# Rows of v from VectorE's 32 by 32 transposes, levels scaled per group, and another order of loads

## What is computed

```python
# cond: weight + LoRA delta, quantised per group of 128 to 8 codebook levels
lora_delta = lora_B @ lora_A * (32.0 / 64)
cb    = codebook / max(|codebook|)
scale = exp(scale_log)                               # (512, 4, 1)
norm  = (weight + lora_delta).reshape(512, 4, 128) / scale
quantized = cb[searchsorted((cb[:-1] + cb[1:]) / 2, norm)]
xc = x @ (quantized * scale + lora_delta).T
# attention, one head of 128, over 128 keys
q, k, v = split(xc @ Wqkv + bqkv)
x = x + (softmax(q @ k.T / sqrt(128)) @ v) @ Wo + bo
# cond2: base product and two of 8 experts of rank 16
logits = x @ Wr.T + 5 * one_hot(language)
gates  = softmax over the top 2 of the logits
m = x @ W.T + 2 * einsum(x @ A, gates, B)
# ffn with an 8-bit weight
out = x + m @ (ffn_scale * (qweight - zero_point)).T + bias
```

## Time and profile before

| | us |
|---|---|
| median of 3 runs | 107.56 (107.47 to 108.09) |
| the profiled execution | 107.76 |
| its span, first to last instruction | 105.8 |
| TensorE busy | 101.3 |
| VectorE busy | 67.9 |
| ScalarE busy | 52.1 |
| POOL busy | 31.8 |

### The profile page before, as it was taken

The page is one execution under the profiler, slowest core; times in us unless marked ns, Lnnn a source line. Parts: engine busy times, 40 slices in busy tenths (PEclk is TensorE's granted clock), DMA queues, the critical chain, the costliest instruction groups (busy, mean ns, idle before and its releaser), DMA issues.

```text
span 105.8 us, 1459 instructions
## 1 busy us (share of the span) xinstructions
PE 101.3 (96%) x513; PEld 84.1 (79%) x513; DVE 67.9 (64%) x163; ACT 52.1 (49%) x92; POOL 31.8 (30%) x40
## 2 busy tenths in 40 slices
PE   6999999999999999999999999999999999999980
PEld 6748568889788899899888786888898888888850
DVE  0199899889999999525999753014946802572441
ACT  4077898999989932934222239272037204002000
POOL 4000246799709570399000056400000400000000
PEclk9999999999999999999999999999999999999999
DMA  1999999960000000000000000000000640000083
GB/s 40 338 344 301 410 400 406 404 253 0 0 3 0 0 0 0 9 0 0 0 0 0 0 0 0 6 0 0 0 0 0 237 160 0 6 0 0 3 297 99
DMA packets 4599, 9.83 MB, mean 93 GB/s; under 512 B 752, under 2 KB 1008, under 8 KB 4592
## 3 DMA queue, kind: packets, MB, share of 16 engines
q1 hardware_dynamic: 4448, 9.48, 24.6%
q10 hardware_dynamic: 144, 0.26, 0.6%
HBM read 7.64 MB, written 2.10 MB: 92 GB/s over the span
## 4 chain that ended last, share of the span: by engine, by line
PE 89%; DMA 4%; DVE 2%; ACT 1%; DVEq 1%; issue 0%
PE psum L860 19%; PE psum L862 19%; PE psum L861 19%; PE psum L885 7%; DMA lora<-in_lora 4%; PE psum L876 3%; PE psum L895 3%; PE psum L910 3%; PE psum L901 3%; PE psum L905 3%; PE psum L1010 2%; PE psum L1031 2%; PE psum L1025 2%; ACT moe L462 1%; PE psum L1017 1%; PE psum L926 1%
## 5 line engine op out<-in xcount | busy, mean ns | idle before, releaser
L662 DVE COPY_PREDICATED cond_work<-cond_work,psum 128x1024 f32<-128x1024 int32 x10 | 13.7, 1366 | 1.1 <-ACT cond_work L363 0.7
L860 PE MATMUL psum<-G_hi,xT_hi 128*128 128x512 f32 x32 | 12.7, 398 | 0.0
L862 PE MATMUL psum<-G_hi,xT_lo 128*128 128x512 f32 x32 | 12.5, 390 | 0.0
L861 PE MATMUL psum<-G_lo,xT_hi 128*128 128x512 f32 x32 | 12.5, 390 | 0.0
L363 ACT ACTIVATE cond_work<-cond_n,cut_bias 128x1024 f32<-128x1024 f32 x10 | 11.2, 1143 | 0.6 <-DVE cond_n L699 0.6
L578 POOL TENSOR_TENSOR hl<-hl,hl_bias 128x272 f32<-128x272 f32 (+2 forms) x4 | 3.1, 774 | 26.4 <-ACT hl L374 14.4
L523 POOL TENSOR_TENSOR xT_lo<-xT,xT_hi 128x1024 fp32r<-128x1024 f32 x4 | 9.6, 2411 | 3.2 <-DVE cond_work L668 3.2
L860 PE MATMUL psum<-xT_hi,split_b_hi 128*128 128x512 f32 x24 | 9.6, 401 | 0.0
L862 PE MATMUL psum<-xT_hi,split_b_lo 128*128 128x512 f32 x24 | 9.4, 391 | 0.0
L861 PE MATMUL psum<-xT_lo,split_b_hi 128*128 128x512 f32 x24 | 9.4, 390 | 0.0
L885 PE MATMUL psum<-hlT,xT 128*128 128x136 f32 x64 | 8.4, 281 | 0.0
(11 more groups left out here) (166 smaller groups left out, 237.4 us busy)
## 6 DMA issues: line engine op xcount, KB each, us to landing
out<-cond_work SPq DMA_DIRECT2D x7, 256.0 KB, 2.1
cond_n<-in_cond_w SPq DMA_DIRECT2D x2, 512.0 KB, 6.6
xT<-in_x_t SPq DMA_DIRECT2D x2, 512.0 KB, 7.6
q_i<-in_q_t SPq DMA_DIRECT2D x4, 256.0 KB, 7.4
moe<-in_moe_w SPq DMA_DIRECT2D x4, 256.0 KB, 7.4
xT<-in_x_t SPq DMA_DIRECT2D x1, 1024.0 KB, 12.4
wqkv_n<-in_wqkv SPq DMA_DIRECT2D x1, 768.0 KB, 10.3
hlT<-in_hl_t SPq DMA_DIRECT2D x1, 272.0 KB, 5.7
```

Source lines behind the costliest of these rows:

```text
L662: dve.copy_predicated(half(level, h), beyond[n % len(beyond)].bitcast(I32), psum[EARLY][:, j + 1:j + 2].to_broadcast([P, 2 * C])).then_inc ...
L860: pe.matmul(out_ap, l_hi, r_hi, start=first, stop=False)
L861: pe.matmul(out_ap, l_hi, r_lo, start=False, stop=False)
L862: return pe.matmul(out_ap, l_lo, r_hi, start=False, stop=last)
```

## The change

- v's rows. TensorE's `v_rows` and ScalarE's `v_out` go. `v_turn` on VectorE makes them from vT with 16 transposes per half, each of one 32-partition quadrant by 32 columns of 4 batches at once, written to another quadrant. Eight of half 0 stand between `softmax_max(0)` and `softmax_norm(0)`, the other 8 and the 16 of half 1 behind it. `attend` waits for them; `qkv(1, 1, 2)` waits for the copy of vT in place of `v_out`.
- Levels. VectorE makes a table of levels times scales (7 x 16) in bank 7 and the lowest row of it, `floor`; `level` starts from it and `pick` overwrites it with scaled levels per group. `w_eff` becomes one add for each 512 columns. `w_eff_lo` of tiles 0 and 1 goes to POOL (`w_eff_rest`).
- Order. q0 and moe0 load ahead of cond_w0, q2 and moe2 ahead of cond_w1. `w_full(0)` stands ahead of `w_delta_first`; `moe_hi`/`w_hi` and `w_lo` move up by one `beyond_cut` or `pick`. `G_first` stands ahead of `x_hl(0)`, whose result goes to bank 6; delta's tiles 2 and 3 go to banks 4 and 5. The 4 idle turns behind delta go. `scores(1)` stands ahead of `y_o(0)`. `expert_no` is set by VectorE in place of POOL.
- The end. The last batch is stored whole.

```diff
-    FILL = 4
+    DELTA_BANKS = (0, 1, 4, 5)
...
             load("small", small[:, :], small_in)
+            load_proj_weights(0)
             load("cond_w0", cond_n[:, 0:2, :], cond_w[:, 0:2, :])
             load("hlT", hlT[:, :, :], hl_t)
             load("x0", xT[:, 0, :, :], x_t[0])
-            load_proj_weights(0)
             load_proj_weights(1)
+            load_proj_weights(2)
             load("cond_w1", cond_n[:, 2:4, :], cond_w[:, 2:4, :])
-            load_proj_weights(2)
             load_proj_weights(3)
...
-            for b in range(BATCH - 1):
+            for b in range(BATCH):
                 sp.wait_ge(y_ready, b + 1)
                 sp.dma_start(out[b], y_out[:, b, :]).then_inc(stored, 16)
-            b = BATCH - 1
-            for n in range(2):
-                sp.wait_ge(y_ready, b + n + 1)
-                s = slice(n * C // 2, (n + 1) * C // 2)
-                sp.dma_start(out[b, :, s], y_out[:, b, s]).then_inc(stored, 16)
...
+        def v_quads(ap, h, n):
+            return ap[:, h, :].rearrange("p (b n) -> p b n", b=TPH)[:, :, n * QUAD:(n + 1) * QUAD]
...
             delta_out(0)
             delta_out(1)
-            set_level()
             delta_out(2)
             delta_out(3)
+            act.wait_ge(floor_ready, 1)
+            act.activation(by_group(half(level, 0)), floor_of(0), ACT.Copy).then_inc(level_set, 1)
             beyond_cut(0, 0)
-            beyond_cut(1, 0)
             moe_hi(1)
             w_hi(1)
-            beyond_cut(2, 0)
-            hl_raw(0, 4)
+            beyond_cut(1, 0)
             moe_hi(2)
             w_hi(2)
-            beyond_cut(3, 0)
+            beyond_cut(2, 0)
+            hl_raw(0, 6)
             moe_hi(3)
             w_hi(3)
+            beyond_cut(3, 0)
...
-                dve.copy_predicated(half(level, h), beyond[n % len(beyond)].bitcast(I32),
-                                    psum[EARLY][:, j + 1:j + 2].to_broadcast([P, 2 * C])).then_inc(picked, 1)
+                at = GROUPS * j + GROUPS // 2 * h
+                dve.copy_predicated(by_group(half(level, h)), by_group(beyond[n % len(beyond)].bitcast(I32)),
+                                    psum[EARLY][:, at:at + GROUPS // 2].unsqueeze(2).to_broadcast(
+                                        [P, GROUPS // 2, P])).then_inc(picked, 1)
...
-                for g in range(CT * o, CT * (o + 1)):
-                    ins = dve.scalar_tensor_tensor(g_block(level, g), g_block(level, g), scale[:, g:g + 1],
-                                                   g_block(delta, g), ALU.mult, ALU.add)
-                ins.then_inc(w_eff_ready, 1)
+                dve.tensor_tensor(level[:, o, :], level[:, o, :], delta[:, o, :], ALU.add).then_inc(w_eff_ready, 1)
...
+            w_full(0)
             w_delta_first()
...
-            w_full(0)
+            w_full(1)
             pick(0, 0)
-            w_full(1)
-            pick(1, 0)
             w_lo(1)
             w_full(2)
-            pick(2, 0)
+            pick(1, 0)
             w_lo(2)
             w_full(3)
+            pick(2, 0)
+            w_lo(3)
             pick(3, 0)
-            w_lo(3)
...
+            def v_turn(h, columns):
+                dve.wait_ge(qkvT_ready, 3 + h)
+                for k in columns:
+                    for d in range(QUADS):
+                        dve.transpose(v_quads(v, h, d)[k * QUAD:(k + 1) * QUAD], v_quads(vT, h, k)[d * QUAD:(d + 1) * QUAD])\
+                           .then_inc(v_ready, 1)
...
             softmax_max(0, 3)
+            v_turn(0, range(0, 2))
             softmax_norm(0)
+            v_turn(0, range(2, QUADS))
+            v_turn(1, range(QUADS))
             o_lo(0)
...
-            idle_turns(FILL)
...
+            G_first()
             pe.wait_ge(loaded["hlT"], 16)
-            x_hl(0, 4)
-            G_first()
+            x_hl(0, 6)
             G_product(1)
...
             qkv(1, 2, 0)
-            pe.wait_ge(qkvT_ready, 3)
-            v_rows(0, 2)
-
...
             probs_turn(0, 3)
-            pe.wait_ge(v_ready, 1)
+            pe.wait_ge(qkvT_ready, 3)
             qkv(1, 1, 2)
...
             o_hl(0, 1, 2)
+            pe.wait_ge(qkvT_ready, 6)
+            scores(1, 0)
             pe.wait_ge(oT_hi_ready, 1)
             pe.wait_ge(oT_lo_ready, 1)
-            y_o(0)
-            pe.wait_ge(qkvT_ready, 6)
-            scores(1, 0)
-            for t in range(1, TPH):
+            for t in range(TPH):
                 y_o(t)
...
             x_hl(3, 3, (6, 7))
-            v_rows(1, 2)
```

More of the change, by code:

```diff
@@ L61, in block_kernel @@
     SOFTMAX_SCALE = float(D) ** -0.5
+    QUAD = 32
+    QUADS = P // QUAD
     LORA_COPIES = 2
@@ L94, in block_kernel @@
         levels = sb("levels", [P, LEVELS])
+        floor = sb("floor", [P, GROUPS])
         cuts = sb("cuts", [P, CUTS])
@@ L251, in block_kernel @@
         max_ready = sem("max_ready")
+        v_ready = sem("v_ready")
         probs_ready = sem("probs_ready")
@@ L346, in w_hi @@
                 rounded(split_b_hi[:, o, :], w_ffn[:, o, :], w_hi_ready)
-            def set_level():
-                act.wait_ge(ones_ready, 1)
-                act.wait_ge(levels_ready, 1)
-                act.activation(half(level, 0), ones[:, 0:1].to_broadcast([P, 2 * C]), ACT.Identity,
-                               bias=levels[:, 0:1], scale=0.0).then_inc(level_set, 1)
             def beyond_cut(j, h):
@@ L528, in _ @@
             pool.memset(ones[:, :], 1.0).then_inc(ones_ready, 1)
-            for e in range(E):
-                pool.memset(expert_no[:, e:e + 1], float(e)).then_inc(ident_ready, 1)
             def x_lo(pair):
@@ L555, in _ @@
                 [P, GROUPS // 2, P]), ALU.mult).then_inc(norm_late_ready, 1)
-            pool.tensor_copy(half(level, 1), levels[:, 0:1].to_broadcast([P, 2 * C])).then_inc(level_late_set, 1)
+            pool.tensor_copy(by_group(half(level, 1)), floor_of(1)).then_inc(level_late_set, 1)
             pool.wait_ge(expb_hi_ready, 1)
@@ L561, in _ @@
             x_lo(1)
+            w_eff_rest(0)
             wqkv_rest(0)
-            pool.wait_ge(w_eff_lo_ready, 2)
+            w_eff_rest(1)
             wqkv_rest(1)
@@ L606, in _ @@
             dve.memset(blank[:, :], 0.0).then_inc(blank_ready, 1)
+            for e in range(E):
+                dve.memset(expert_no[:, e:e + 1], float(e)).then_inc(expert_no_ready, 1)
             dve.wait_ge(loaded["small"], 16)
@@ L618, in _ @@
             dve.wait_ge(scale_ready, 1)
+            dve.tensor_scalar(floor[:, :], scale, levels[:, 0:1], None, ALU.mult).then_inc(floor_ready, 1)
             dve.reciprocal(inv_scale[:, :], scale).then_inc(inv_scale_ready, 1)
@@ L693, in _ @@
             alone(dve.tensor_tensor(cuts[:, 2:3], cuts[:, 2:3], cuts[:, 3:4], ALU.min))
+            dve.tensor_tensor(psum[EARLY][:, 0:CUTS * GROUPS].rearrange("p (j g) -> p j g", j=CUTS),
+                              levels[:, 1:LEVELS].unsqueeze(2).to_broadcast([P, CUTS, GROUPS]),
+                              scale.unsqueeze(1).to_broadcast([P, CUTS, GROUPS]), ALU.mult).then_inc(picks_ready, 1)
             dve.tensor_scalar(cut_bias[:, :], cuts[:, :], -CUT_GAIN, None, ALU.mult).then_inc(cut_bias_ready, 1)
+            w_full(0)
             w_delta_first()
@@ L725, in _ @@
             pick(3, 1)
-            w_eff_lo(0)
-            w_eff_lo(1)
             pick(4, 1)
@@ L832, in gh_lo, with y_store @@
                    .then_inc(ghT_lo_ready, 1)
-            def y_store(t, n=slice(0, C)):
+            def y_store(t):
                 dve.wait_ge(y_done, t + 1)
                 dve.wait_ge(y_bias_ready, 1)
-                dve.tensor_tensor(y_out[:, t, n], psum[4 + t % 4][:, n], y_bias[:, n], ALU.add).then_inc(y_ready, 1)
+                dve.tensor_tensor(y_out[:, t, :], psum[4 + t % 4][:, :], y_bias[:, :], ALU.add).then_inc(y_ready, 1)
             softmax_max(0, 3)
+            v_turn(0, range(0, 2))
             softmax_norm(0)
+            v_turn(0, range(2, QUADS))
+            v_turn(1, range(QUADS))
             o_lo(0)
@@ L850, in _ @@
             gh_lo(1, 0)
-            for t in range(TPH, BATCH - 1):
+            for t in range(TPH, BATCH):
                 y_store(t)
-            for n in range(2):
-                y_store(BATCH - 1, slice(n * C // 2, (n + 1) * C // 2))
         @block.tensor
@@ L875, in _ @@
             for o in range(CT):
-                pe.matmul(psum[o][:, :], lora[:, 0, o * P:(o + 1) * P], lora[:, 1, :], start=True, stop=True)\
+                pe.matmul(psum[DELTA_BANKS[o]][:, :], lora[:, 0, o * P:(o + 1) * P], lora[:, 1, :], start=True, stop=True)\
                   .then_inc(delta_done, 1)
-            idle_turns(FILL)
             def x_hl(part, bank, batches=None, base=0):
@@ L1000, in _ @@
             pe.wait_ge(ident_ready, 1)
-            def v_rows(h, bank):
-                for b in range(TPH):
-                    mm = pe.transpose(psum[bank][:, b * P:(b + 1) * P], vT[:, h, b * P:(b + 1) * P], ident[:, :])
```

(1 more changed line is left out.)

42 lines of the change are left out of this document (22 added, 20 removed).

## The result

| | before | after |
|---|---|---|
| median in the timed comparison, us | 107.83 (107.47 to 108.54) | 111.02 (110.75 to 111.16) |
| the profiled execution | 107.76 | 110.75 |
| its span | 105.8 | 108.9 |
| VectorE busy | 67.9 | 76.6 |
| granted clock, mean | 1.00 | 0.984 |

What follows compares the result with a forecast made beforehand. TensorE was taken to bound the kernel nearly everywhere, except in the softmax stretch. The terms -0.1 (start, behind softmax), -0.44 (second v transposes) and +0.1 (end) gave -0.45 us: 107.56 to 107.1 us, range 106.3 to 108.0.

Steps and rivals of the forecast that it cites:

- Step 2: Softmax stage, half 0: eight VectorE transposes at 0.29 us each in 1.58 us idle; probabilities turned at 65.3, not 65.40.
- what is left of step 1 behind step 2: Sum's term at probs_turn(0): of the 0.85 us gained at the start, only 0.1 remains after the softmax stage, so -0.1.
- Step 1: Kernel start: without idle turns G_first begins at 8.31, 0.89 us gained, inputs in time; scores(0) 0.85 us early, at 59.4.
- VectorE becomes the bound of the stage: Rival, softmax_max(0) to o_lo(0): dearer transposes delay reciprocal and gating; 108.2 us at 0.35, 110.8 at 0.43; chance 0.1.
- rule on quadrants: Softmax stage: instructions starting in another quadrant wait for all earlier ones; with 311 ns a transpose, no gain there, sum 107.3.
- Step 3: Second v transposes, between x_hl and y_gh(0) on TensorE's dense line: the whole 0.44 us gained, no wait at y_gh(0).
- Step 4: The end: one whole store in place of two half stores lands at 105.55 in place of 105.45; 0.1 us lost.

Runs made afterwards that it cites:

- kernel 1: After, with both halves' v transposes back on TensorE and ScalarE's copies behind them, rest of the change kept; 107.63 us, ratio 0.9962.
- kernel 2: Before, with only the v transposes moved to VectorE (8, scaling, 24); loads, levels, idle turns and last store as before; 110.87 us, ratio 1.0232.
- kernel 7: After, with 4 transposes in place of 8 ahead of softmax_norm(0), the others behind it; 108.84 us, ratio 1.0069.
- kernel 6: kernel 3 with 16 more VectorE transposes behind its 16, reading and writing quadrant 0 alone, result unused; 107.58 us in one run.
- kernel 8: kernel 3 with moe_lo's four products of G_product(1) ahead of w_lo's; 107.43 us, ratio 0.9926.
- kernel 3: After, with half 0's v transposes back on TensorE and half 1's 16 on VectorE behind the scaling; 107.35 us, ratio 0.9923.
- kernel 4: After, with 12 idle turns of TensorE in the gap ahead of probs_turn(0); 109.19 us, ratio 1.0086.
- kernel 5: After, with POOL's addition of y_bias made to wait until the scaling of the probabilities is done; 108.12 us, ratio 1.000.

## Why the prediction was wrong, step by step

**Step 2 failed, in its price and in what it left out.** The place was right: the softmax chain sets the stage, and the transposes count from 0.197 us each on. The price was 0.29 us "that is no overlap"; it is 0.33. The duration was nearly met (303 ns against 292 from the line through the earlier trace rows), but instructions that don't overlap have a further 0.03 us between them. By the step's own rule the eight cost 2.65 in place of 2.32 us, 0.3 of the loss, and would have turned the probabilities at about 65.6 in place of 65.3 had TensorE come to the stage as forecast, which makes 107.4. The price of 0.33 was inside my bounds of 0.21 to 0.35, so that alone would have left the time within the range. In the sum the term "what is left of step 1 behind step 2" stood at -0.1; at probs_turn(0) it measured +1.85, and with the clock, which the sum lacks, +3.46 at attend(0).

The larger part was in no step. In the stage's sum the scaling was moved as a block of 0.69 us, and what POOL does at that moment wasn't looked at. Two edits brought the two together. The eight transposes moved the scaling 0.8 us later. And the addition moved 0.67 us earlier: 0.2 of it with the whole stage (it begins at 65.86 in kernel 1), and 0.47 since it waits for ScalarE's boG, in front of which the change took away v_rows(0) and v_out(0), ScalarE's copy of v. That is one more consequence I had not followed. The timelines of before and then of after:

```profile
64.68 0.72 POOL L581 TENSOR_TENSOR hl<-hl,lang_hot 128x8 f32<-128x8 f32 x1
65.38 0.60 ACT L497 ACTIVATE boG<-psum 128x512 f32<-128x512 f32 x1
66.06 1.29 POOL L589 TENSOR_TENSOR ffn_bias_bc<-boG,ffn_bias_bc 128x512 f32<-128x512 f32 x1 [0.66 <-ACT boG L497]
```

```profile
64.72 0.59 ACT L493 ACTIVATE boG<-psum 128x512 f32<-128x512 f32 x1
```

Before, the scaling was over at 65.35 and the addition began at 66.06. (Kernel 2 has lost v_out(0) as well, and meets the addition in the same way. In kernel 7, without v_out(0) but with an early scaling, they don't meet. Late transposes with v_out(0) left in were not run.) The trace of before even held two signs that one of these engines can hold up the other. One is the first row above, an operation on 8 columns that begins 0.03 us behind VectorE's scaling and takes 0.72 us; in after, with no scaling beside it, it takes 0.20. The other is w_lo, 0.67 and 0.69 us at its other two places, and 1.01 here beside POOL:

```profile
16.25 1.01 DVE L644 TENSOR_TENSOR split_b_lo<-q_i,split_b_hi 128x512 fp32r<-128x512 f32 x1
```

It is the later one that waits. POOL's subtraction beside this w_lo ran from 15.40 to 16.71, and w_lo ended at 17.26, 0.55 us behind it. The scaling of after ended at 67.20, 0.55 us behind POOL's 66.65, and w_lo(1) of kernel 1 (below) at 14.90, 0.54 us behind 14.36. So these traces give an estimate: a two-input VectorE instruction of this size that begins during one of POOL's ends some 0.55 us after POOL does. That would have given the 1.05 us beforehand.

Then the gap of 2.61 us, its 1.05 from the collision, lowered the clock: another 1.61 us. Neither had a term, a rival or a bound. The stage's prices were bounded one instruction at a time, and that left out what two together do.

**The rival "VectorE becomes the bound of the stage"** had the place and the sign, but the wrong mechanism: it wanted 0.35 to 0.43 us a transpose to reach 108.2 or 110.8, and it got there at 0.33 with the collision and the clock. Its second half held as a threshold: "from 0.32 us the 24 behind the scaling pass the 7.5 + 0.93 us that gating(0) has". In after o_lo(0) starts at 75.26 right behind the last transpose, and gating(0) starts 9.1 us after probs_turn in place of 7.5. It did no harm there, since TensorE was late itself: y_gh(0) comes +3.14 late where attend(0) came +3.46. In kernel 7, where TensorE was on time, that queue did cost (0.23 us at o_lo(0)).

**Of the Trainium skill's rule on quadrants** ("VectorE: DVE Perf Modes", section "Two Vector instructions with no wait between them"), which the prediction put beside 311 ns and a time of 107.3: kernel 6 bears it out for this machine. Starts in another quadrant don't overlap (0.33 against 0.196 us). One takes 303 ns, near the 311 that the page has for another shape. That price was nearer than my middle value, but a sum with it still comes out level with before: the rule doesn't reach the other 2.7 us of the loss.

**Step 1 was half right, and its gain hardly shows in after.** Its order works: G_first follows the lora products with no idle turns between, and none of its inputs is late in after (where the lora products end sooner, in kernels 1, 7 and 8, its first weights wait for w_full(0), and it loses 0.1 us). But scores(0) came only 0.19 us earlier, not 0.85. The start of after (timeline), and of before behind it:

```profile
4.71 0.50 PEld L884 LDWEIGHTS psum<-lora 128*128 128x128 f32 x2 [0.60 <-DMA lora<-in_lora]
...
4.74 4.51 PE L884 MATMUL psum<-lora 128*128 128x512 f32 x8 [0.33 <-DMA lora<-in_lora]
...
9.08 3.60 PE L903 MATMUL psum<-q_i,moe 128*128 128x512 f32 x8
...
14.28 1.18 PE L909 MATMUL psum<-split_b_hi,split_a_hi 128*128 128x512 f32 x4
```

```profile
4.64 3.67 PE L876 MATMUL psum<-lora 128*128 128x512 f32 x8 [0.23 <-DMA lora<-in_lora]
```

The same eight lora products took 4.51 us here and 3.67 in before's profile, as the first few went at a slower rate: the first two weight loads took 0.50 us together and the third 0.34, where before's profile has 0.30 and 0.19; from the fourth on they take 0.19 here too. So G_first began at 9.08, not 8.31. That isn't the change's doing: a slow start (4.45 to 4.75 us) is in profiles of both orders (after and kernels 2, 3 and 4), and a fast one too (3.67 us in before and kernels 1, 7 and 8); kernels 5 and 6 lie between, 3.79 and 3.95. Like with like, at the slow start, softmax's maximum stands at 62.24 in kernel 2 (before's order) and at 61.22 in after: 1.02 us gained. Of this, 0.12 is kernel 2's still slower lora products (4.64 us; they end at 9.20, in after at 9.08), so 0.90 is the order's, just the 0.89 of the step. At the fast start it is 61.41 in before and 61.23 in kernel 1, only 0.18. There half of the gain is gone behind the G products (x_hl(1) starts at 22.80, in before at 23.18), and another 0.2 by scores(0). The first place is G_product(1):

```profile
8.80 1.23 DVE L658 TENSOR_TENSOR cond_n<-cond_n,delta 128x1024 f32<-128x1024 f32 x1 [0.72 <-DMA cond_n<-in_cond_w]
...
13.07 1.29 POOL L526 TENSOR_TENSOR split_a_lo<-moe,split_a_hi 128x512 fp32r<-128x512 f32 x1 [11.45 <-ACT split_a_hi L342]
13.74 1.16 DVE L652 TENSOR_TENSOR split_b_lo<-q_i,split_b_hi 128x512 fp32r<-128x512 f32 x1
...
14.96 0.19 PEld L918 LDWEIGHTS psum<-split_b_lo,split_a_hi 128*128 128x128 f32 x1 [0.58 <-DVE split_b_lo L652]
```

(Timeline of kernel 1.) Two things meet there. cond_w0 lands late: w_delta_first waits for it until 8.80, where step 1 had 8.45, and all of VectorE's queue moves with it, so that w_lo(1) begins at 13.74, in after at 13.31. And the collision is here too: w_lo(1) takes 1.16 us beside POOL's 1.29. Its products start 1.31 us behind the first of G_product(1), in after 1.02, so TensorE loses 0.3 us (the 0.58 of the row is the idle time of the weight loads). In after and kernel 8 w_lo(1) is as slow, but early enough. Step 1 had named 0.3 us as the smallest slack, "all of this fits", and cond_w0's landing at 8.4; in kernels 1, 3, 4, 6 and 7 VectorE waits for cond_w0 until 8.8 to 9.1. With cond_w0 late a fast start gains nothing in the new order: scores(0) stands at 60.06 in kernel 1 (fast) and at 60.05 in after (slow, cond_w0 in time). Where both are in time, step 1 comes out: scores(0) at 59.48 in kernel 8 and 59.59 in kernel 5, against its 59.4. The median of kernel 1, 0.4% below before, lies between what the two cases give (0.2 and 0.9%).

**Steps 3 and 4.** Step 3 held: y_gh(0) starts with no wait, and the 0.44 us is part of the table's -0.32 (gh_turn, just ahead of it, starts 3.58 us later than before, 81.33 against the earlier trace rows, y_gh(0) 3.14). Step 4 didn't show its 0.1 us: from the last addition (105.83) to the end are 3.07 us, before 3.10.

```profile
83.54 0.48 PE L868 MATMUL psum<-Bf_hi,split_a_hi 128*128 128x512 f32 x1
...
105.83 0.69 DVE L844 TENSOR_TENSOR cond_work<-psum,ffn_bias_bc 128x512 f32<-128x512 f32 x1 [1.40 <-PE psum L870]
```

**The sum as measured:** -0.19 (start) + 0.99 (transposes) + 1.05 (collision) + 1.61 (clock) - 0.32 (v_rows gone, less 0.12 of small drifts) = +3.14 us, against the forecast -0.45.

## What to carry to other kernels

When an instruction moves on VectorE, look at which POOL instruction it will stand beside. A VectorE instruction with two SBUF inputs that began during one of POOL's was held up by nearly the rest of it here (1.05 us of 1.19), and a wait that costs nothing on POOL's queue was worth 2.9 us. A longer gap on TensorE isn't paid once: add the time that the clock needs to come back, or fill the gap, or keep it at a length that a run has borne (1.60 us in kernel 5). Work moved onto an engine because it idles on average needs a place in its queue, and a row of instructions that walks over the quadrants cost its full duration and a little more for each (0.33 us for 303 ns).
